# Layer-norm statistics of a Mamba block on ScalarE by row sums, in place of VectorE's statistics instructions

## The reference, cut to what matters

```
x1 = LN(x + mamba(x))            # mamba(x) = out_proj(y * silu(z)) + x
out = LN(x1 + moe(x1))

LN(v) = (v - mean(v)) / sqrt(var(v) + 1e-5)        # over the 128 features
mamba: h = (x - mean) / sqrt(var + 1e-6) * gamma + beta
       u, z = in_proj(h); uc = silu(conv4(u)); dt, B, C = x_proj(uc)
       delta = softplus(dt_proj(dt)); A = -exp(A_log)
       state[d,n] = exp(delta[d] * A[d,n]) * state[d,n] + delta[d] * B[n] * uc[d]
       y[d] = sum_n state[d,n] * C[n] + uc[d] * D[d]         # 256 channels, 16 states
moe:   8 experts of 128 -> 512 -> 128 with gelu, the best two of each token
```

## Time and profile before

| | |
|---|---|
| device time, median of 3 runs | 922.57 us (919.72 to 924.37) |
| the profiled execution's own time | 926.12 us |
| its span, first to last instruction | 924.2 us |
| busy: PE / DVE / ACT / POOL | 606.1 / 650.0 / 447.8 / 612.5 us |
| prologue, up to DVE's first inflow | 67.08 us |
| main loop: one unit in the middle | 74.3 us |

### The profile page before, as it was taken

The page is one execution under the profiler, slowest core; times in us unless marked ns, Lnnn a source line. Parts: engine busy times, 40 slices in busy tenths (PEclk is TensorE's granted clock), DMA queues, the critical chain, the costliest instruction groups (busy, mean ns, idle before and its releaser), DMA issues. The chain is left out here.

```text
span 924.2 us, 11664 instructions
## 1 busy us (share of the span) xinstructions
PE 606.1 (66%) x2666; PEld 294.8 (32%) x2666; DVE 650.0 (70%) x998; ACT 447.8 (48%) x908; POOL 612.5 (66%) x628
## 2 busy tenths in 40 slices
PE   4766757768767777675875755756417889888700
PEld 2221111312222232131232121221207778777700
DVE  2037888989998998998998899999432333333353
ACT  3536656474654746736557444334103444444323
POOL 5024476585797797797978789877753655556544
PEclk8775687776686686697577665565556999999955
DMA  3057438376666876657557646862015666666463
GB/s 79 0 126 175 99 91 194 92 170 137 140 165 158 226 166 144 142 135 177 116 132 160 143 113 160 193 147 68 30 60 143 185 172 180 173 177 188 122 183 89
DMA packets 76338, 128.22 MB, mean 139 GB/s; under 512 B 10544, under 2 KB 53488, under 8 KB 68080
## 3 DMA queue, kind: packets, MB, share of 16 engines
q1 hardware_dynamic: 71920, 118.43, 53.0%
q0 software_dynamic: 4352, 9.05, 3.2%
HBM read 102.64 MB, written 18.51 MB: 131 GB/s over the span
## 5 line engine op out<-in xcount | busy, mean ns | idle before, releaser
L517 POOL TENSOR_TENSOR hc<-hs,Crep 128x1024 f32<-128x1024 f32 x128 | 308.3, 2409 | 116.6 <-DVE hs L1263 91.0
L1263 DVE TENSOR_TENSOR_SCAN hs<-bank,state,flow 128x512 f32<-128x512 f32 x256 | 314.7, 1269 | 42.4 <-ACT bank L1033 36.4
L1033 ACT ACTIVATE bank<-bank,negA 128x512 f32<-128x512 f32 x256 | 167.0, 660 | 175.2 <-PE bank L740 171.5
L740 PE MATMUL bank<-dparts,sel 96*128 96x512 bf16 x256 | 128.7, 512 | 134.9 <-DVE hs L1263 127.8
L1253 DVE TENSOR_TENSOR flow<-flow,bank 128x2048 f32<-128x2048 f32 x64 | 145.2, 2269 | 13.7 <-issue 12.3
L740 PEld LDWEIGHTS bank<-dparts,sel 96*128 96x128 bf16 x256 | 27.5, 109 | 315.0 <-DVE hs L1263 263.2
L1185 ACT ACTIVATE flow<-bank,b1T 128x128 f32<-128x128 f32 x288 | 82.2, 369 | 88.7 <-PE bank L914 77.2
L749 PE MATMUL bank<-hc,kc 128*32 128x512 f32 x512 | 98.9, 856 | 18.3 <-DVE yg L1271 14.7
L914 PE MATMUL bank<-flow 128*128 128x128 f32 x576 | 82.9, 288 | 23.4 <-issue 15.2
L639 POOL DMA_INDIRECT results<-flow,idn x72 | 72.2, 1003 | 33.8 <-issue 32.0
L698 PE MATMUL bank<-hT,wtapT 128*128 128x512 f32 x128 | 77.0, 742 | 14.6 <-ACT hT L969 10.8
(11 more groups left out here) (168 smaller groups left out, 806.1 us busy)
## 6 DMA issues: line engine op xcount, KB each, us to landing
flow<-du_d SPq DMA_DIRECT2D x64, 1024.0 KB
flow<-L_ffn_W SPq DMA_DIRECT2D x72, 256.0 KB
dparts<-part SPq DMA_DIRECT2D x96, 64.0 KB
xg<-xs SPq DMA_DIRECT2D x72, 66.0 KB, 2.6
du_d<-du SPq DMA_DIRECT2D x32, 128.0 KB, 2.3
hs<-results SPq DMA_DIRECT2D x16, 256.0 KB, 3.5
xin<-L_attn_x SPq DMA_DIRECT2D x8, 256.0 KB, 3.0
spill<-xn SPq DMA_DIRECT2D x8, 256.0 KB
```

Of the source, the lines that this page charges most:

```text
L517: nc.gpsimd.tensor_tensor(hc[:, Q % 2, two, :], hs[:, Q % 2, two, :], Crep[u % 2][:].unsqueeze(1).broadcast_to([P, 2, T]), ALU.mult).then_ ...
L740: nc.tensor.matmul(dbank[G % 3][:], sel[:, g // 4 % 4, :], dparts[u % 2][:, 4 * (g // 16) + g % 4, :])\
L1033: nc.scalar.activation(dbank[G % 3][:], dbank[G % 3][:], ACT.Exp, scale=negA[:, ch:ch + 1]).then_inc(s_ex, 1)
L1263: nc.vector.tensor_tensor_scan(hs[:, Q % 2, j, :], dbank[G % 3][:], flow[Q % 3][:, j, :], state[:, Q // QUADS % 2, Q % QUADS, j:j + 1], AL ...
```

## The change: statistics by row sums on ScalarE

DVE no longer takes statistics for the front and the back norm. ACT does it in two passes over the four tiles, each a group of four ACTIVATE of 128x128 with a row sum as a second output (`accum_out`): first the sum of the values, then, with the negated mean as bias, the sum of the squares of the deviations. Between the two POOL turns the sum into the negated mean (one small instruction), and behind the second it makes `veps`, `rstd` and `nmr` as before. The elementwise outputs of the passes are not used: they are written to `xhat` (front) and to a new bf16 tile `bjunk` (back).

New and moved work, by place:

```diff
 # ScalarE
+def front_sums(u):                 # waits for x(u) and for xhat to be free
+    for t in range(TT):
+        ins = nc.scalar.activation(xhat[:, t, :], xin[u % 4][:, t, :], ACT.Identity, accum_out=fsum[:, t:t + 1])
+    ins.then_inc(s_fst, 1)
+def front_squares(u):
+    act.wait_ge(s_fnm, u + 1)
+    after(act, s_frs, 3 * u)
+    for t in range(TT):
+        ins = nc.scalar.activation(xhat[:, t, :], xin[u % 4][:, t, :], ACT.Square, bias=nmean[:, t:t + 1],
+                                   accum_out=fsq[:, t:t + 1])
+    ins.then_inc(s_fag, 1)
 # back_sums and back_squares: the same on res, into bsum and bsq, with bjunk as output
...
+                    if g == 17 and j >= 1:
+                        back_sums(j - 1)
+                    if g == 19 and j >= 1:
+                        back_squares(j - 1)
                     if g == 23 and j >= 1:
                         xns(j - 1)
+                    if g == 27 and j + 3 < UNITS:
+                        front_sums(j + 3)
+                    if g == 0 and j >= 1 and j + 2 < UNITS:
+                        front_squares(j + 2)
+                    if g == 3 and j == 0:
+                        front_sums(2)
+                    if g == 7 and j == 0:
+                        front_squares(2)
...
+            front_sums(0)
+            front_squares(0)
             xhats(0)
...
             setup()
+            front_sums(1)
+            front_squares(1)
             xhats(1)
...
+            back_sums(last)
+            back_squares(last)
             xns(last)
 # GpSimd
-                    if j >= 1 and slot == 0 and j + 2 < UNITS:
+                    if slot == (2 if j else 4) and j + 2 < UNITS:
                         front_rstd(j + 2)
                     if j == 0 and slot == 2:
-                        front_rstd(2)
+                        front_mean(2)
+                    if slot == 14 and j + 3 < UNITS:
+                        front_mean(j + 3)
+                    if slot == 8 and j >= 1:
+                        back_mean(j - 1)
...
-                    if slot == 9 and j >= 1:
+                    if slot == 10 and j >= 1:
                         back_rstd(j - 1)
...
+            front_mean(0)
             front_rstd(0)
+            front_mean(1)
             front_rstd(1)
...
+            back_mean(last)
             back_rstd(last)
 # VectorE: front_stats(0), (1), (2), front_stats(j + 3) at g == 27,
 # back_stats(j - 1) at g == 16 and back_stats(last) are gone
```

More of the change, by code:

```diff
@@ L98, in mamba_moe @@
         xin = [sb(f"xin{r}", [P, TT, D]) for r in range(4)]
-        bst = sb("bst", [P, TT, 6])
-        mv = sb("mv", [P, TT, 2])
+        fsum = sb("fsum", [P, TT])
+        fsq = sb("fsq", [P, TT])
         minus_half = sb("minus_half", [P, TT])
@@ L140, in mamba_moe @@
         res = sb("res", [P, TT, D])
-        cst = sb("cst", [P, TT, 6])
-        cmv = sb("cmv", [P, TT, 2])
+        bjunk = sb("bjunk", [P, TT, D], BF16)
+        bsum = sb("bsum", [P, TT])
+        bsq = sb("bsq", [P, TT])
         cveps = sb("cveps", [P, TT])
@@ L225, in mamba_moe @@
         s_x = [sem(f"x_loaded{r}") for r in range(4)]
-        s_fst = sem("front_stats")
-        s_fag = sem("front_aggr")
+        s_fst = sem("front_sums")
+        s_fnm = sem("front_mean_negated")
+        s_fag = sem("front_squares")
         s_frs = sem("front_rstd")
@@ L261, in mamba_moe @@
         s_md = sem("m_bank_drained")
-        s_cst = sem("ln1_stats")
-        s_cag = sem("ln1_aggr")
+        s_cst = sem("ln1_sums")
+        s_cnm = sem("ln1_mean_negated")
+        s_cag = sem("ln1_squares")
         s_crs = sem("ln1_rstd")
@@ L482, in rsqrt, with front_mean @@
                 nc.gpsimd.tensor_tensor(product[:], nm[:], rs[:], ALU.mult).then_inc(done, 1)
+            def front_mean(u):
+                pool.wait_ge(s_fst, u + 1)
+                after(pool, s_frs, 3 * u)
+                nc.gpsimd.tensor_scalar(nmean[:], fsum[:], -1.0 / D, None, ALU.mult).then_inc(s_fnm, 1)
             def front_rstd(u):
@@ L486, in front_rstd, with back_mean @@
                 after(pool, s_xh, u)
-                rsqrt(veps, rstd, nmean, nmr, mv, 1e-6, s_frs, u)
+                nc.gpsimd.tensor_scalar(veps[:], fsq[:], 1.0 / D, 1e-6, ALU.mult, ALU.add).then_inc(s_frs, 1)
+                pool.wait_ge(s_frs, 3 * u + 1)
+                nc.gpsimd.tensor_tensor(rstd[:], veps[:], minus_half[:], ALU.pow).then_inc(s_frs, 1)
+                pool.wait_ge(s_frs, 3 * u + 2)
+                nc.gpsimd.tensor_tensor(nmr[:], nmean[:], rstd[:], ALU.mult).then_inc(s_frs, 1)
+            def back_mean(u):
+                pool.wait_ge(s_cst, u + 1)
+                after(pool, s_crs, 3 * u)
+                nc.gpsimd.tensor_scalar(cnmean[:], bsum[:], -1.0 / D, None, ALU.mult).then_inc(s_cnm, 1)
             def back_rstd(u):
@@ L491, in back_rstd @@
                 after(pool, s_xn, u)
-                rsqrt(cveps, crstd, cnmean, cnmr, cmv, 1e-5, s_crs, u)
+                nc.gpsimd.tensor_scalar(cveps[:], bsq[:], 1.0 / D, 1e-5, ALU.mult, ALU.add).then_inc(s_crs, 1)
+                pool.wait_ge(s_crs, 3 * u + 1)
+                nc.gpsimd.tensor_tensor(crstd[:], cveps[:], minus_half[:], ALU.pow).then_inc(s_crs, 1)
+                pool.wait_ge(s_crs, 3 * u + 2)
+                nc.gpsimd.tensor_tensor(cnmr[:], cnmean[:], crstd[:], ALU.mult).then_inc(s_crs, 1)
             def add_relu(u):
@@ L955, in filled, with back_sums, back_squares @@
                 return fbank[f % 2]
+            def front_sums(u):
+                act.wait_ge(s_x[u % 4], 16 * (u // 4 + 1))
+                after(act, s_fag, u)
+                if u:
+                    act.wait_ge(s_ff, fill_of(u - 1, "T") + 1)
+                for t in range(TT):
[8 more added lines that the diff above has]
+                ins.then_inc(s_fag, 1)
+            def back_sums(u):
+                act.wait_ge(s_md, 4 * u + 1)
+                after(act, s_cag, u)
+                for t in range(TT):
+                    ins = nc.scalar.activation(bjunk[:, t, :], res[:, t, :], ACT.Identity, accum_out=bsum[:, t:t + 1])
+                ins.then_inc(s_cst, 1)
+            def back_squares(u):
+                act.wait_ge(s_cnm, u + 1)
+                after(act, s_crs, 3 * u)
+                for t in range(TT):
+                    ins = nc.scalar.activation(bjunk[:, t, :], res[:, t, :], ACT.Square, bias=cnmean[:, t:t + 1],
+                                               accum_out=bsq[:, t:t + 1])
+                ins.then_inc(s_cag, 1)
             def xhats(u):
-                act.wait_ge(s_frs, 4 * u + 4)
+                act.wait_ge(s_frs, 3 * u + 3)
                 after(act, s_ff, 9 * (u - 1) + 1 if u else 0)
@@ L1213, in moments @@
                 ins.then_inc(s2, 1)
-            def front_stats(u):
-                dve.wait_ge(s_x[u % 4], 16 * (u // 4 + 1))
-                after(dve, s_frs, 4 * u)
-                moments(bst, xin[u % 4], mv, s_fst, s_fag, u)
-            front_stats(0)
             dve.wait_ge(s_w, 16 * 12)
@@ L1278, in residual @@
                                                ALU.mult, ALU.add).then_inc(s_md, 1)
-            def back_stats(u):
-                dve.wait_ge(s_md, 4 * u + 1)
-                after(dve, s_crs, 4 * u)
-                moments(cst, res, cmv, s_cst, s_cag, u)
             def best_two(u):
@@ L1335, in host @@
                     scan(STEPS * j + g)
-                    if j == 0 and g == 3:
-                        front_stats(2)
                     if g == 5 and j >= 2:
@@ L1347, in host @@
                         residual(j - 1)
-                    if g == 16 and j >= 1:
-                        back_stats(j - 1)
                     if g == du_at and late:
@@ L1353, in host @@
                         post(j, 0)
-                    if g == 27 and j + 3 < UNITS:
-                        front_stats(j + 3)
                     if g == 30 and j >= 1:
@@ L1371, in _ @@
             residual(last)
-            back_stats(last)
             best_two(last)
```

3 lines of the change are left out of this document (1 added, 2 removed).

## The result

The changed kernel takes 947.1 us (median; 942.9 to 949.5), the kernel before 921.5 us (919.7 to 924.4) in runs on the same chip. The ratio is 1.027, with a 95% interval of 1.022 to 1.032: slower by 25.6 us on the medians. The forecast was 961 with a range of 942 to 978. The profiled executions stand at 946.9 us (span 945.1) and 926.1 us (span 924.2), so the traces show 20.9 us; the other 4.7 are that the traced execution of before lay above its own median.

The account below looks back on a forecast made before the run. DVE was taken to bound the main loop, the chain ACT, POOL, PE the prologue. Terms 10.7 + 3.4 + 18.5 + 2.5 + 2.8 = 37.9 us slower gave 961 on the median, range 942 to 978.

Parts of the forecast that it names:

- dear read-out: Rival: reading out the sum also stops overlap between neighbouring passes, a block is 3 us; 50 us more, 972; chance 0.17.
- the block: One ACT pass over four tiles with row sums: taken as 2.0 us, between 1.25 and 2.4.
- loop that breaks even: Rival: POOL's slots start earlier and ACT catches up, only prologue and ends cost; 14 to 20 us, 940; chance 0.15.
- Relief in full: Rival: all 16.0 us of DVE's relief come off the loop; no change, or 916 at B = 1.25; chance 0.06.
- prologue: Before the loop: unit 1's blocks and chain delay `sel`, so PE starts the convolution 10.7 us later.
- first unit: First loop unit: squares at step 7 and sums at step 27 delay ACT, against 2.46 us of DVE saved; +3.4.
- units 2 to 6: Middle units: front norm +2.8, back norm +2.3, less 1.2 and 0.2 saved; 3.7 per unit, 18.5 in five.
- units 7 and 8: No silu or front norm: scan 24 waits about 2.4 us, less 1.2; +1.2 each, 2.5 together.
- last unit's end: Two blocks, a mean and the chain replace 1.23 us of statistics, all on the path; +2.8.
- expert part: The expert part: as before, no change.
- upper end: Block of 2.4 us, if writing out each sum is a small instruction of 194 ns; total 42 us, 965.
- The marks: Signs in middle units: scan 9 waits 3.5 to 4 us, scan 25 waits 4 or more; a unit of 78 us.

Follow-up runs that it names:

- experiment 4: Changed kernel with `sel` ahead of unit 1's mean and chain, POOL's front chain in slot 0, back chain in slot 9: 915.3 us, ratio 0.990 to the kernel before.
- experiment 5: Kernel before, with DVE's cast of the expert indices written as a two-input maximum of the indices with themselves: 922.7 us, ratio 1.000.
- 10: Kernel before, with POOL writing `sel` right behind the identity, ahead of all norm work: 920.5 us, ratio 0.997.
- experiment 11: Kernel before, with DVE's cast of the expert indices and the two operations behind it moved behind the next unit's scan 0: 919.8 us, ratio 0.997.

## Why the prediction was right, and where its sizes were off

**The mechanism held.** Slower, because small statistics that pass from ACT through POOL and back to ACT stand in front of decays that DVE already waits for, and in the prologue in front of `sel`, which PE waits for. Shown by moves alone: the three that the forecast's own steps point at (`sel` behind unit 1's chain, `front_rstd` behind slot 2, `back_rstd` in slot 10) took 9.7, 19.7 and 7.3 us off, and all of them 31.8, to below the kernel before.

**Rivals.** The dear read-out (972) is refuted by the block: 1.28 to 1.65, not 3. The loop that breaks even (940) is refuted by the waits, 72.1 against 36.4, though the total, 947, lies between it and the forecast. That it falls within the range at all is owed to the room left for this rival: by itself the forecast was 950 to 970, and its sum gives 953 at the cheapest block. Relief in full (916) was held for unlikely as `xhats` and `xns` would wait for POOL; they did, by 17.7 and 23.5 us. Where the moves let these chains come early the kernel takes 913 to 915, near that rival's own number. Of its own condition the rival was right. A further one, not put, that ScalarE's greater load by itself makes the kernel slow, falls by experiment 4.

**The sum's terms.** By the traces:

```
term                          forecast   measured
prologue                        10.7        9.2   (8.0 to the convolution, 1.2 PE's clock)
first unit                       3.4        0.6
units 2 to 6                    18.5       14.1   (20.6 with the cast's 6.5 put back)
units 7 and 8                    2.5       -1.8
last unit's end                  2.8        1.6
expert part                      0         -3.1
sum                             37.9       20.9   (the parts are rounded)
```

Of the 17 us between the two sums the largest part is the cast's 6.5, a term that the forecast put at nothing; units 7 and 8 are 4.3, the expert part 3.1, the first unit 2.8, the prologue 1.5 and the last unit's end 1.2, less 2.1 by which the middle units grew more than forecast.

The term of the sum that was itself mis-sized is the block: taken as 2.0 us "since a second output that needs writing is the likelier case", measured at 1.28 and 1.65, a mean of 1.46. By the forecast's own sign this is near to wrong ("far from 2 us"). The lower bound, 1.25, came from `xhats` less one operand; the squares, which have one pointer operand, took 0.39 a pass, what `xhats` takes with two and no sum, and the sums, with none, 0.29. A pointer costs about 0.1 us, and so does the read-out, and the two cancel. The forecast took the sums for passes with one operand, but they have none. It also tied its upper end to ScalarE taking two instructions for a pass with a sum: it does take two, and the upper end doesn't follow, as half of the second is hidden. Two of each stand in the prologue, 5.9 us for 8.0, which is 2.1 of its 2.7 too much to the convolution. ACT's busy time rose by 42 us and not 64 for the same reason.

In the first unit the scans' waits for ACT rose by 3.1 us (14.2 to 17.3), against 2.46 of statistics saved; the forecast had let them rise by 5.9. The squares at step 7 and the sums at step 27 are 0.35 and 0.72 short of 2 us, and more of them than thought lay in ACT's own waits for PE in front of decays, which fell from 22.7 to 17.0 us in that unit.

In units 2 to 6 the front norm's +2.8 and the back norm's +2.3 came as 0.9 at scan 8 and 2.06 at scan 9, and as 1.7 at scan 24 and 1.0 at scan 25. The marks said 3.5 to 4 for scan 9 and 4 or more for scan 25: the delay was right and was split over two scans, of which the forecast looked only at the second. The unit of 78 us came as 76.1, and the difference is mostly the cast. That 6.5 us was missing from the forecast altogether: the row was in the trace, at 1079 ns mean for 128x8, and what makes it long is a product of POOL that begins at its start, which this change shifts.

Units 7 and 8 together lost nothing. Scan 24 waits 1.7 us in both, where the forecast had 2.4, and unit 8 grew by 1.0, near the 1.2 forecast. But in unit 7 the kernel before had a wait of 3.0 us at scan 2, behind the copy of C, which was gone after; the forecast had no term for it. The expert part's -3.1 is no effect of the change: that part took 252.0 us in the profiled execution of before, and 247.8 to 250.6 in those of all the other kernels, three of which (5, 10 and 11) have the statistics of before. The traced execution of before lay 4.7 us above its median, so part of the forecast's overshoot is the same thing: on the medians the change costs 25.6. One rival's sum has a slip that changes nothing: the dear read-out, at blocks of 3 us, counts 2 us for units 7 and 8, less than the 2.5 at blocks of 2.

## What to carry to other kernels

A statistic of four numbers per partition costs its engine little; what it costs the kernel is set by where its two handovers stand in three in-order queues. Before moving such work to the less loaded engine, find for each handover the instruction that waits behind it and whether that one has slack already: the same instructions in other places of their queues were worth 34 us here, from 2.7% slower to 1.1% faster. And look for small operations with means far above their size: here they showed a hold by another engine, which any change of the loop may move to another unit or to the next operation. Before a gain is put down to such a shift, count all the operations that can be held: here the cast was free and the one two places behind it was caught.

## What the runs showed of the hardware

- An ACTIVATE with a row sum is two instructions: its own and a read of the accumulator of 0.19 us, which overlaps by half with the neighbours. Net 0.09 us per pass of 128 columns (0.91 to 1.28 us, and 1.28 to 1.65, per four).
- Some small DVE operations with all their data in SBUF don't finish while a POOL product of 2.35 us runs. A cast or a maximum over 128x8 (0.15 us alone) took 2.3 to 2.8 us, `oh`, a comparison with two inputs (0.23 alone), 2.4 to 3.0, and `taken`, a sum of two inputs (0.19 alone), 2.9 to 3.1, each ending within 0.1 us of the product, and at least one of them is in every kernel's trace. It holds too where the DVE operation began up to 0.7 us ahead of the product; there POOL's indirect DMA was running. Eight scalings of 128x128 took 4.11 us beside POOL's fills and 1.66 apart from them.
- Others aren't held: of the BN_STATS on tiles in SBUF, 16 lie wholly inside a POOL product in the trace of before and took 0.27 to 0.28 us as elsewhere, and MAX8, FIND_INDEX8 and a reduction there took 0.15 to 0.20. Scans that read their decays from a bank and run beside the same products keep their 1.25 to 1.29 us.
- It goes the other way too: where DVE's `du`, a product of two tiles in SBUF over 128x1024 (1.20 us), began 0.18 us ahead of POOL's product of slot 8 (at 412.44 in the unit of the earlier trace rows), that product took 3.23 us in place of 2.35, and so in seven units of the eight.
- PE's granted clock differs between executions over the same work, and it moves the first inflow. In three executions whose prologue is the same code (experiment 11, before, experiment 5) the convolution started at 18.17, 18.29 and 18.20, the clock granted between 18 and 67 us was 0.67, 0.71 and 0.83, and the first inflow came at 68.5, 67.1 and 64.9. A gain of 1 or 2 us in this prologue is not to be read from one trace.
